# A fused transformer block on one core: another order of the weight pieces in the first image's front, and four fillers in place of eight

## The reference

```
x = x + conv_ref(_gn(x))       # xs = spike(x); q, k, v = spike(bn(W xs)); kv = k^T v per head; p-projection
t = to_tokens(x)
t = t + attn_ref(_ln_t(t))     # 6 heads, causal softmax over 1024 tokens
t = t + ffn_ref(_ln_t(t))      # 4 experts 192 -> 768 -> 192, gelu, top 2 of 4 by gate
x = from_tokens(t)
```

## Time and profile before

| | |
|---|---|
| median of 3 runs | 1661.14 us (1660.44 to 1661.31) |
| profiled execution, its own time | 1659.74 us |
| its span | 1657.7 us |
| PE, DVE, ACT, POOL busy | 1586.3, 1188.0, 904.0, 173.5 us |
| mean granted clock of PE | 0.996 |

### The profile page before, as it was taken

One profiled execution on the slowest core, in us unless ns is written; L12 is line 12 of the kernel. 1 busy time (PEld: TensorE's weight loads), 2 busy tenths in 40 slices (PEclk: granted clock), 3 DMA queues, 4 the chain that ended last, 5 costly groups with the idle time before them and its releaser, 6 DMA issues.

```text
span 1657.7 us, 32908 instructions
## 1 busy us (share of the span) xinstructions
PE 1586.3 (96%) x13274; PEld 1034.4 (62%) x13274; DVE 1188.0 (72%) x2537; ACT 904.0 (55%) x1329; POOL 173.5 (10%) x247
## 2 busy tenths in 40 slices
PE   3989999999999999999999999999999999999999
PEld 1534676657665576656766567665776557765676
DVE  6687786767776776867768678676777777686644
ACT  3217654466545665466554665446654566545665
POOL 2200102001210003000020010200121000300000
PEclk9999999999999999999999999999999999999999
DMA  4202002100111002010020100200011100200000
GB/s 162 59 25 65 1 1 68 35 16 2 41 28 49 1 1 68 1 49 1 1 68 1 50 2 1 67 26 25 1 38 32 49 1 1 68 1 11 1 11 10
DMA packets 25131, 47.30 MB, mean 29 GB/s; under 512 B 7410, under 2 KB 16946, under 8 KB 23700
## 3 DMA queue, kind: packets, MB, share of 16 engines
q1 hardware_dynamic: 15728, 27.85, 6.1%
q0 software_dynamic: 6144, 9.45, 2.4%
q10 hardware_dynamic: 3108, 7.91, 1.3%
HBM read 19.82 MB, written 6.29 MB: 16 GB/s over the span
## 4 chain that ended last, share of the span: by engine, by line
PE 73%; DVE 17%; ACT 5%; issue 2%; POOL 1%; DMA 1%; SPq 0%; DVEq 0%; ACTq 0%; POOLq 0%
PE ps L440 22%; PE ps L732 18%; PE ps L677 10%; PE ps L475 6%; DVE mx L1174 4%; PE ps L618 4%; PE ps L524 3%; DVE room L1361 3%; PE ps L447 2%; ACT room L900 2%; DVE norm_stats L1015 2%; ACT room L908 2%; DVE acc L1345 1%; PE ps L511 1%; PE ps L479 1%
## 5 line engine op out<-in xcount | busy, mean ns | idle before, releaser
L900 ACT ACTIVATE room<-ps,b_sb 128x512 f32<-128x512 f32 x384 | 263.1, 685 | 438.5 <-PE ps L440 438.4
L732 PE MATMUL ps<-wout_h,room 128*128 128x192 f16 x3072 | 457.2, 246 | 0.0
L1361 DVE SCALAR_TENSOR_TENSOR room<-room 128x512 f16<-128x512 f32 x384 | 263.2, 689 | 183.0 <-ACT room L908 180.8
L732 PE MATMUL ps<-wout_l,room 128*128 128x192 f16 x1536 | 377.4, 246 | 0.0
L732 PEld LDWEIGHTS ps<-wout_h,room 128*128 128x128 f16 x3072 | 285.9, 98 | 34.0 <-issue 3.2
L880 ACT ACTIVATE room<-ps 128x1024 f32<-128x1024 f32 (+3 forms) x288 | 224.8, 811 | 141.4 <-PE ps L479 104.0
L1174 DVE TENSOR_REDUCE mx<-ps 128x2 f32<-128x1024 f32 (+3 forms) x288 | 265.8, 953 | 33.7 <-PE ps L622 21.1
L908 ACT ACTIVATE room<-room 128x512 f16<-128x512 f32 x384 | 241.9, 630 | 33.6 <-PE ps L732 0.4
L677 PE MATMUL ps<-room,v 128*64 128x512 f32 (+3 forms) x1152 | 231.7, 486 | 0.9 <-DVE o L1306 0.9
L618 PE MATMUL ps<-qk 96*128 96x512 f16 (+3 forms) x576 | 151.0, 329 | 17.4 <-DVE mx L1174 10.6
L732 PEld LDWEIGHTS ps<-wout_l,room 128*128 128x128 f16 x1536 | 150.1, 98 | 27.1
(11 more groups left out here) (203 smaller groups left out, 2317.4 us busy)
## 6 DMA issues: line engine op xcount, KB each, us to landing
xc<-x_ch SPq DMA_DIRECT2D x8, 768.0 KB, 5.8
qk<-qk_all SPq DMA_DIRECT2D x96, 64.0 KB, 2.3
qk<-qk_all POOLq DMA_DIRECT2D x96, 64.0 KB, 2.5
out<-acc ACTq DMA_DIRECT2D x16, 384.0 KB, 2.6
xt<-x_tok SPq DMA_DIRECT2D x7, 768.0 KB, 7.1
qk<-qk_all POOLq DMA_DIRECT2D x96, 32.0 KB, 2.0
qk<-qk_all SPq DMA_DIRECT2D x96, 32.0 KB, 2.3
room<-w_in SPq DMA_DIRECT2D x2, 1024.0 KB, 8.5
```

Source lines behind the costliest of these rows:

```text
L732: mm = pe.matmul(dst, hid[:, s, tok], w[:, n, :], start=(k == 0 and m == 0 and t % 2 == 0), stop=False, skip_group_check=True)
L900: act.activation(h32[:, i % N_H, :], ps[:, H_BANK[i], :], ACT.Gelu, scale=1 / (U_SCALE * W_SCALE), bias=b1_sb[:, n:n + 1])\
L1361: V.scalar_tensor_tensor(out=h_l[:, s, :], in0=h32[:, s, :], scalar=A_SCALE, in1=h_h[:, s, :], op0=ALU.mult, op1=ALU.subtract)\
```

## The change

The pieces are ordered by column block, so H0, T0, H1, T1, O2. DVE's places between the pieces move to `PIECE_AT = (10, 21.5, 29, 29, 30.5)`, ACT has places of its own, `HIGH_AT`. PE waits at the transposition for two pieces and not for five, and ACT waits for all five before it writes into the room that the slots share with `attend`. Four fillers stand before kvm and before attn.

```diff
-PIECE_AT = (10, 12, 14, 16, 18)
+PIECE_AT = (10, 21.5, 29, 29, 30.5)
+HIGH_AT = (0, 16, 16, 28, 28)
 LATER_AT = (6, 18)
 PER_CHUNK = 2.25
-IDLE = {"kvm": 8, "attn": 8, "p": 4, "turn": 28, "qk": 4, "first maximum": 16}
+IDLE = {"kvm": 4, "attn": 4, "p": 4, "turn": 28, "qk": 4, "first maximum": 16}
...
-        pieces = [(kind, c0, min(W, IN_COLS - c0)) for kind in ("head", "tail")
-                  for c0 in range(0, IN_COLS, W)]
+        pieces = [(kind, c0, min(W, IN_COLS - c0)) for c0 in range(0, IN_COLS, W)
+                  for kind in ("head", "tail")]
+        n_first = 2
...
-            pe.wait_ge(stage_lo, len(pieces))
+            pe.wait_ge(stage_lo, n_first)
...
-                if n:
-                    first.until(PIECE_AT[n])
+                first.until(HIGH_AT[n])
             act.wait_ge(late_in, 16 * n_late)
             first.finish()
+            act.wait_ge(stage_lo, len(pieces))
             attend(0)
```

## The result

The changed kernel takes 1667.38 us (median of 6 runs, 1666.04 to 1667.87); the kernel before took 1660.07 us in the runs beside it. The ratio is 1.0043, with a 95% interval of 1.0031 to 1.0055: slower by 7.3 us. The profiled execution has a span of 1665.4 us, 7.7 more than before.

A forecast was written before the change was run, and what follows sets the result against it. PE was taken as full after image 0's front; -0.1 (first query) + 0.3 (landing) + 2.0 (first maximum) = +2.2 us on 1659.74 gave 1661.9, and the median 1.4 above gave 1663.3; eight in ten from 1659 to 1667.

The forecast's parts named there:

- SP's queue: Later load and queries wait until T1 is split: 5.5 us lost, first query at 72.85 us, practically as before.
- the landing behind 1 MB: Block 0's queries land later because the 1 MB load goes ahead in SP's queue: 0.3 us, between 0 and 1.
- The early gain: Front of image 0 up to attn: kvm at 39.25 us, attn about 8.9 us earlier.
- H1's split beside the power: DVE's split between `norm_var` and `norm_tmp` delays POOL's power: 1.55 us lost, between 0 and 1.83.
- The clock at the transposition: PE's clock falls after a 3.3 us gap before the transposition: 0 to 2.9 us lost, taken as 1.6.
- The half rate at the first maxima: Fillers no longer cover PE's wait, so the first maxima run at half clock: 2.0 us lost.
- The stretch at 98 us: Half-rate stretch already in the kernel before, worth some 1.4 us; whether it returns was open, so left in place.
- The slower one: Rival: half rate also in the spiking convolutions, or long stretches at transposition and maxima; +6.7 us, 1667.9; chance 0.27.
- a fall of the clock at 37 to 41 us: PE's thin work there lets the clock fall, so attn and p cost 1.5 to 2 us more.
- The second rival: No overlap problem beside the power, no clock fall at the transposition: lead 8.9 us, 1659 to 1660 us; chance 0.13.
- the lead kept: Rival: SP's wait does not hold the queries, or keys set the landing; 1652 to 1655 us; chance 0.07.

The follow-up runs named there:

- ACT's wait alone: The kernel before with only ACT's wait for all five pieces added before the first exponential; 1664.36 us, ratio 1.0021.
- O2 beside the power: The kernel before with the split of O2 (512 columns) moved between the layer norm's variance and the use of its power; 1666.08 us in one run.
- the fillers alone: The kernel before with four fillers before kvm and four before attn in place of eight; 1660.12 us, ratio 0.9996.
- the early split: The changed kernel with H1's split moved from beside the layer norm's power to step 17.5, right behind kv's split; 1666.66 us, ratio 1.0035.
- all three repairs: The changed kernel with ACT's wait ahead of the maxima's rows, the later load behind both blocks' queries, and H1's split at 17.5; 1653.88 us, ratio 0.9960.

## Why the prediction was wrong

**The step that failed: a line of the change was never costed.** The prediction goes through the pieces, DVE's places, SP's queue and the fillers, and says nothing on the added `act.wait_ge(stage_lo, len(pieces))`. Left out of a sum it stands there at nothing, with the silent reason that all pieces are long split by then. The premise that only image 0's front is touched hides it too: the line stands behind the front, at the start of `attend`. They are, and the wait still costs: 1.28 us of table load and 1.6 us of clock behind it, 2.9 in the profiles, and 0.6 more in images 3 and 7. By the medians moving it gives back 3.4, and adding it alone costs 4.1 (3.5 by the ratio). That it could be seen ahead without a time: in the order on ACT the table load had gained a wait, and the trace of before had its 1.28 us and its idle 20 us behind it. The Trainium skill (ScalarE: Activation LUTs, "What ACT_TABLE_LOAD costs") gives 1283 ns for the load, which the trace agrees with, and some 1380 ns more for a drain, which it does not show: the exponential starts at 125.34, 0.01 us after the load's end at 125.33, and in the kernel before the load at 98.73 follows the end of the instruction ahead of it by 0.01.

**The term that was mis-sized: the landing behind 1 MB.** It was put at 0.3, between 0 and 1, from the rate of a single load, with the twelve issues leaving room for it. It measured 2.6 (84.95 against 82.36, with the last issue where it was). The direction was right and the upper end too low. The transfers' table has a median of 4.6 us over the twelve queries of 64 KB, so at least half of them were late and not the first alone.

**What held.** The early gain: kvm at 39.66 and attn at 41.70 for 39.25 and 41.2, 8.4 for 8.9. The missing 0.5 is not in the kernel but in the execution: the run with the wait moved has the same front, its q products come to full pace at 29.65 us instead of 31.47, and it starts kvm at 39.19 and attn at 41.23, as predicted. The place that the gain is counted from moves as much: kvm at 47.66 in the kernel before, at 46.69 in the run with ACT's wait alone. H1's split beside the power: 1.51 for 1.55, the pause 3.20 for 3.3; the three powers of 3.17 us beside 1.82 of split, 2.03 beside 0.68 and 1.65 without one are what the lock of the port pair in the Trainium skill (SBUF — State Buffer, "Who interferes with whom") leads one to expect. The clock at the transposition: 1.1 (6.85 to 5.75 of lead) for 1.6. SP's queue: first query 72.76 for 72.85, and the run with the load behind the queries shows that the order of issues alone turns the kernel from slower to faster. The half rate at the first maxima: 1.5 (2.6 to 4.1) for 2.0; the fillers take it away. Its price was read loosely: the stretch at 98 us is put at 1.2 in one place and at 1.4 in another, while PE is busy throughout it, so that 3.4 us at half rate are 1.7 us of its work; and how much of that reaches DVE no row says. The stretch at 98 us came again, at about 103, and changed nothing in the difference (+4.1 before it, +4.25 after), so leaving it in place was right.

The account: 2.2 forecast, 2.3 more for the landing, 2.9 for ACT's wait, 0.5 less for the half rate at the maxima and 0.6 that appear only in images 3 and 7 give 7.5, against 7.7 between the two profiles and 7.3 between the medians. The early gain and the clock at the transposition were each 0.5 off and cancel; that the first query's time was met to 0.1 us is luck. The forecast of 1663.3 also started from 1661.14 for the kernel before, which took 1660.07 in the runs beside the changed one. So the time misses by 4.1, the difference between the kernels by 5.1.

**The rivals.** The slower one was given at 1667.9, and the time came out beside it, but not by its mechanism. It wanted two of three to go badly: a fall of the clock at 37 to 41 us, 2.9 at the transposition and 3.5 at the maxima. The clock is 1.00 from 36 to 58 us, and the other two cost 1.1 and 1.5. Its places were wrong, although a clock's fall elsewhere (behind the table load, 1.6) was a third of the 5.1 us that were missing. The second rival, no fall and no overlap problem, fell with the power of 3.17 us. The first, the lead kept, is what the kernel becomes when load and wait are moved: 1654.49 us in its range of 1652 to 1655. With only the load moved, which is all that this rival names, it is 1657.62.

**Still open.** The 0.6 us in images 3 and 7 belong to the added wait: all ten profiles of kernels with that line have both steps, wherever the line stands, and the three without it (the kernel before, O2 beside the power, the fillers alone) have neither. Why it shifts a place hundreds of microseconds later is not known. Nor is it settled when a pause makes the clock fall: 1.69 us before the transposition did nothing in the profile of the kernel before, and 1.69 or 1.68 us brought it down in four others (ACT's wait alone, the early split, the fillers alone, all three repairs), the first of them with the same front. So it differs from execution to execution, and one profile against another can't tell differences under about 1 us there. How the landing grows between 256 KB and 1 MB was not tried.

## What to carry to other kernels

A wait that is always met in time can still cost: look in the order of the instructions on which one it, and the wait that was there, now stand, above all where an activation table is loaded. A wait by count in an in-order queue of transfers ties everything behind it to the work that is counted, so when that work moves, the queue has to be reordered too, large loads that nobody needs yet going last. A lead won early is worth only what the last of the joining paths gives, and fillers sized for the old waits have to be sized again when it moves.

## What the runs showed of the hardware

A second wait ahead of an exponential moved its table load from 98.73 to 120.25 us, and one wait on a condition met long before cost 3.5 us (ratio 1.0021, 1.0012 to 1.0030; 4.1 by the medians). A megabyte ahead of the queries in SP's queue lengthened their landing from 2.3 to 4.6 us in the median, a quarter of it by nothing, and the keys of POOL's own queue took 4.9 and 2.0. And the same pause of PE, 1.69 us, in the same front, was followed once by a clock of 1.00 and once by 0.62: the transposition came 0.94 us earlier in the second, and the first query left 0.36 later. Last, the first q products of 512 columns ran 0.43 us apart for 4 to 6 us, half of the full pace, while the column of the granted clock reads 1.00.
